# Dividing the attention output on GpSimd instead of VectorE, with a second copy of the transposed input and a new order at the end of each step

## The reference

```
x = x + attention(layernorm(x))       # 16 heads of 64, causal, own layernorm with weights inside
x = x + ffn(layernorm(x))             # sigmoid encoder, router over 8 experts (top 2), experts, decoder
attention: q, k, v = x Wq + bq, x Wk + bk, x Wv + bv
           p = softmax(q k^T / 8, causal);  z = p v;  out = z Wo + bo
```

## Time and profile before

| | |
|---|---|
| median of 3 runs | 1163.17 us (1163.03 to 1163.51) |
| profiled execution | 1161.71 us, its span 1160.0 us |
| TensorE, VectorE, ScalarE, GpSimd busy | 90%, 78%, 61%, 57% of the span |
| TensorE clock granted, mean | 0.975 |
| DMA, share of 16 engines | 64.3% on the one queue used |

### The profile page before, as it was taken

The page is one execution under the profiler, slowest core; times in us unless marked ns, Lnnn a source line. Parts: engine busy times, 40 slices in busy tenths (PEclk is TensorE's granted clock), DMA queues, the critical chain, the costliest instruction groups (busy, mean ns, idle before and its releaser), DMA issues.

```text
span 1160.0 us, 51334 instructions
## 1 busy us (share of the span) xinstructions
PE 1039.1 (90%) x19852; PEld 772.4 (67%) x19852; DVE 903.1 (78%) x2180; ACT 703.5 (61%) x1474; POOL 658.7 (57%) x658
## 2 busy tenths in 40 slices
PE   5689999999999999999999999999999848699984
PEld 3577777777777777777777777777777636354542
DVE  6878888888888888888888888888888863547573
ACT  4656666666666666666666666666666542577664
POOL 5766666666656666666666666665666202244644
PEclk9999999999999999999999999999999877899998
DMA  7677777777777776777777777777777740132422
GB/s 172 164 182 172 174 169 173 169 173 172 171 167 181 165 175 168 168 168 168 168 170 174 175 172 170 171 169 172 173 173 170 179 91 21 38 84 47 91 50 60
DMA packets 127279, 173.06 MB, mean 149 GB/s; under 512 B 46096, under 2 KB 57360, under 8 KB 127248
## 3 DMA queue, kind: packets, MB, share of 16 engines
q1 hardware_dynamic: 127248, 172.67, 64.3%
HBM read 117.67 MB, written 21.36 MB: 120 GB/s over the span
## 4 chain that ended last, share of the span: by engine, by line
PE 71%; DVE 13%; DMA 5%; issue 5%; ACT 3%; SPq 2%; POOL 1%; DVEq 0%; POOLq 0%; ACTq 0%
PE ZB L658 25%; PE SPS L641 12%; PE SPS L642 10%; PE ZB L626 8%; DVE PTZ L918 4%; PE ZB L631 4%; DMA XTB<-xt_scratch 4%; PE ZB L666 3%; DVE SSB L975 2%; SPq L416 2%; PE SPS L817 1%; PE SPS L791 1%; PE ZB L832 1%; PE ZB L826 1%; PE ZB L809 1%
## 5 line engine op out<-in xcount | busy, mean ns | idle before, releaser
L975 DVE CUSTOM_DVE_ANT_0 SSB<-SPS,MASK 128x640 f32<-128x640 f32 (+7 forms) x512 | 372.0, 745 | 124.6 <-PE SPS L642 111.1
L641 PE MATMUL SPS<-KHP,QS 128*128 (+2 forms) x768 | 326.2, 430 | 33.5 <-DVE NM L975 28.7
L658 PE MATMUL ZB<-PTZ,VR 32*64 32x256 f32 (+2 forms) x16384 | 322.7, 295 | 21.4 <-DVE PTZ L918 19.0
L1278 ACT ACTIVATE PRL<-SSB,NM 128x640 f32<-128x640 f32 (+3 forms) x256 | 253.3, 989 | 144.9 <-DVE NM L975 144.4
L658 PEld LDWEIGHTS ZB<-PTZ,VR 32*64 32x64 f32 x16384 | 271.5, 131 | 69.3 <-issue 53.9
L483 POOL TENSOR_TENSOR X<-X,OT 128x512 f32 (+1 forms) x64 | 81.9, 1279 | 342.3 <-ACT OT L1288 333.9
L642 PE MATMUL SPS<-KLP,QS 128*128 (+2 forms) x768 | 261.4, 348 | 0.0
L918 DVE STREAM_TRANSPOSE PTZ<-PRL 128x640 f32<-128x640 f32 (+3 forms) x256 | 258.6, 1030 | 0.0
L1278 ACT ACTIVATE PRS<-SSB,NM 128x128 f32<-128x128 f32 (+3 forms) x256 | 142.5, 559 | 154.4 <-DVE NM L975 154.4
L641 PEld LDWEIGHTS SPS<-KHP,QS 128*128 128x128 f32 x768 | 145.3, 189 | 110.9 <-issue 47.2
L466 POOL TENSOR_TENSOR QS<-RAW,QS 64x512 fp32r<-64x512 f32 x128 | 165.3, 1292 | 10.3
(11 more groups left out here) (167 smaller groups left out, 999.6 us busy)
## 6 DMA issues: line engine op xcount, KB each, us to landing
VR<-v_scratch SPq DMA_DIRECT2D x256, 256.0 KB, 5.6
KHP<-KHP SPq DMA_DIRECT2D x64, 256.0 KB, 3.2
KLP<-KLP SPq DMA_DIRECT2D x64, 256.0 KB, 3.9
v_scratch<-V SPq DMA_DIRECT2D x32, 512.0 KB, 7.7
RSB<-rcp_scratch SPq DMA_DIRECT2D x64, 256.0 KB, 4.0
XTB<-xt_scratch SPq DMA_DIRECT2D x62, 256.0 KB, 3.4
VR<-gate_scratch SPq DMA_DIRECT2D x16, 512.0 KB, 5.9
WQK<-in_W_q SPq DMA_DIRECT2D x33, 64.0 KB, 3.2
```

Source lines behind the costliest of these rows:

```text
L641: pe.matmul(SP_[n % 2][:, c0:c0 + wc], q, kh[:, c0:c0 + wc], start=True, stop=False)
L658: last = pe.matmul(ZB[h * DH:(h + 1) * DH, i, kt * TR:QT * TR], VR[rows, j, kt, h * DH:(h + 1) * DH], turned_block(h, kt, j, rows), start= ...
L975: v.tensor_tensor_reduce(out=SSB[n % 2][:, 0:w], in0=SP_[n % 2][:, 0:w], in1=MASK[:, S - w:S], scale=1.0, scalar=BIG, op0=ALU.add, op1=ALU ...
L1278: act.activation(exps_of(n), SSB[n % 2][:, 0:w], ACT.Exp, bias=NM[:, col:col + 1], scale=-1.0, accum_out=L[:, col:col + 1]).then_inc(exp_d ...
```

## The change

- The division: ScalarE copies Z from PSUM to the ZN tiles in two copies of 128x512 (`act_z`, after the exponential of unit 11), and GpSimd multiplies ZN by RSB in place in two operations of 128x512 (`divide`, ahead of `add_out(0)`). `out_of(g)` waits for division g only; `v_of` waits for the first copy. The four VectorE operations go.
- V of the step ahead is computed from its own copy of the transposed input, XW, from step 2 on; a transfer of 512 KB a step is added for it (`stage_xv`), ahead of the reciprocals in the queue. XTB's transfers move ahead of V's first spread and wait only for the queries and keys computed from XTB.
- The reciprocals' second transfer also waits for `split_q` of the step, which stands behind the division that read RSB.
- TensorE: `v_of(0)`, `v_of(1)` after scores 13, then scores 14 and 15, then the output products (before: scores 13 and 14, V, output, scores 15).
- VectorE: turn 8 ahead of mask 11 (before: behind it), mask 15 ahead of turn 12, turn 13 of the step behind ahead of mask 0.
- ScalarE: the first output copy after the exponential of unit 14, the second after that of unit 15 (before: after those of 13 and 14, with the exponential of 15 in the next step behind the first evacuation of `qk`).

```diff
+        def stage_xv(sp, it):
+            sp.wait_ge(v_filled, it * 2)
+            sp.nop(nofuse=True)
+            sp.dma_start(XW[:, :], xt_dram[:, bass.ds(((it // HP) % B) * S, S)]).then_inc(xv_staged, DMA)
 ...
+            if isinstance(it, int) and it == STEPS - 1:
+                sp.wait_ge(zn_done, it * 2)
+            else:
+                sp.wait_ge(q_split, it * 4 + 8)
 ...
+        def divide(gp, it, g):
+            gp.wait_ge(z_copied, it * 2 + 2)
+            gp.wait_ge(r_spread, it * (2 * DMA) + 2 * DMA)
+            gp.nop(nofuse=True)
+            z = ZN[g].rearrange("p (t i r) -> p i t r", i=P // TR, r=TR)
+            gp.tensor_tensor(z, z, RSB[:, g, :].rearrange("p (i t r) -> p i t r", t=TC, r=TR), ALU.mult).then_inc(zn_done, 1)
 ...
                 if not first:
+                    divide(gp, it - 1, 0)
+                    divide(gp, it - 1, 1)
                     add_out(gp, it - 1, 0)
 ...
-            scores(13, 14)
+            scores(13)
             v_of(0)
             v_of(1)
+            scores(14, 15)
             out_of(0)
             out_of(1)
-            scores(15)
 ...
-            turn(6, 7)
+            turn(6, 7, 8)
             stats(5)
             mask(11)
-            turn(8)
             mask(12)
 ...
-            for k in range(4):
-                zn(k)
             turn(9)
 ...
             mask(14)
+            mask(15)
             turn(12)
-            mask(15)
 ...
+        def act_z(act, it, k):
+            banks = slice(2 - k * 2, 4 - k * 2)
+            act.wait_ge(pv_done, it * QT + QT)
+            act.activation(PTZ[:, QT * 9 * P:QT * 9 * P + 2 * CH].rearrange("p (q i r) -> p i q r", i=P // TR, r=TR)[:, banks],
+                           ZB[:, banks, 0:QT * TR].rearrange("p i (q r) -> p i q r", r=TR), ACT.Copy).then_inc(z_copied, 1)
 ...
-            exps_to(11, 13)
+            exps_to(11, 12)
+            if not first:
+                act_z(act, it - 1, 0)
+                act_z(act, it - 1, 1)
+            exps_to(12, 13)
             v_of(0)
             exps_to(13, 14)
             v_of(1)
-            out_of(0)
             exps_to(14, 15)
+            out_of(0)
+            exps_to(15, 16)
             out_of(1)
```

More of the change, by code:

```diff
@@ L214, in build_program @@
         x_staged = [sem(f"x_staged{c}") for c in range(2)]
+        xv_staged = sem("xv_staged")
         keys_spread = [sem(f"keys_spread{c}") for c in range(2)]
@@ L222, in build_program @@
         v_early = sem("v_early"); v_late = sem("v_late")
-        pv_done = sem("pv_done"); zn_done = sem("zn_done")
+        pv_done = sem("pv_done"); z_copied = sem("z_copied"); zn_done = sem("zn_done")
         bias_filled = sem("bias_filled"); bias_ready = sem("bias_ready")
@@ L287, in stage_x @@
             part = bass.ds(((it // HP) % B) * S + c * CH, CH)
-            sp.wait_ge(v_filled, it * 2 + c - 1)
+            if isinstance(it, int) and it == 2:
+                sp.wait_ge(v_filled, 3 + c)
+            else:
+                sp.wait_ge(qk_filled, it * 4)
+                sp.nop(nofuse=True)
+            sp.dma_start(XTB[:, c * CH:(c + 1) * CH], xt_dram[:, part]).then_inc(x_staged[c], DMA)
+        def stage_xv(sp, it):
+            sp.wait_ge(v_filled, it * 2)
             sp.nop(nofuse=True)
-            sp.dma_start(XTB[:, c * CH:(c + 1) * CH], xt_dram[:, part]).then_inc(x_staged[c], DMA)
+            sp.dma_start(XW[:, :], xt_dram[:, bass.ds(((it // HP) % B) * S, S)]).then_inc(xv_staged, DMA)
         def stage(sp, it):
@@ L368, in body @@
                 else:
+                    if not last:
+                        stage_xv(sp, it + 1)
                     spread_sums(sp, it - 1)
@@ L378, in body @@
                     spread(sp, it + 1, 1 - par, 1)
+                    if not first:
+                        stage_x(sp, it + 2, 0)
+                        stage_x(sp, it + 2, 1)
                 spread_v(sp, it, half, par, 0)
-                if not last:
+                if first:
                     stage_x(sp, it + 2, 0)
@@ L574, in _ @@
             norm_in(1, 1)
+            divide(gp, STEPS - 1, 0)
+            divide(gp, STEPS - 1, 1)
             add_out(gp, STEPS - 1, 0)
@@ L628, in pe_v @@
         def pe_v(pe, it, s, bank):
+            xt = XTB if isinstance(it, int) and it < 2 else XW
             for k in range(TC):
                 t = s * TC + k
-                last = pe.matmul(bank[:, k * P:(k + 1) * P], XTB[:, t * P:(t + 1) * P],
+                last = pe.matmul(bank[:, k * P:(k + 1) * P], xt[:, t * P:(t + 1) * P],
                                  WV[:, bass.ds((it % HP) * 2, 2), :].rearrange("p h e -> p (h e)"), start=True, stop=True)
@@ L663, in pe_out @@
         def pe_out(pe, it, g, bank):
-            pe.wait_ge(zn_done, it * 4 + 4)
+            pe.wait_ge(zn_done, it * 2 + g + 1)
             for i in range(TC):
@@ L710, in v_of @@
                 else:
-                    pe.wait_ge(zn_done, it * 4 - 2)
+                    pe.wait_ge(z_copied, it * 2 - 1)
+                    if s == 0:
+                        pe.wait_ge(xv_staged, it * DMA)
                 pe_v(pe, it + 1, s, ZB[:, 2 + s, :])
@@ L925, in dve_reciprocal @@
             v.transpose(RT[:, :, :].rearrange("p g c -> p (g c)"), RCP[:, :, :].rearrange("p g c -> p (g c)")).then_inc(rcp_turned, 1)
[L927 to L934, removed]
         def dve_bias(v):
@@ L1036, in back @@
                     dve_reciprocal(v, it - 1, 1 - par)
-            def zn(k):
-                if not first:
-                    dve_zn(v, it - 1, k)
+            turn_back(13)
             mask(0)
@@ L1048, in dve_step @@
                 v.memset(ONES, 1.0).then_inc(zeroed, 1)
-            turn_back(13)
             turn_back(14)
@@ L1210, in _ @@
             dve_low(v, 0, 0)
-            for k in range(4):
-                dve_zn(v, it, k)
             gates_1(v, 0)
@@ L1319, in act_step @@
                 qk(0)
-                act_exp(act, it - 1, 1 - par, UNITS - 1)
                 exps_to(0, 1)
@@ L1350, in act_step @@
             exps_to(14, 15)
+            out_of(0)
+            exps_to(15, 16)
             out_of(1)
-            if last:
-                act_exp(act, it, par, UNITS - 1)
         @block.scalar
@@ L1431, in _ @@
             turn_of(1)
+            act_z(act, STEPS - 1, 0)
+            act_z(act, STEPS - 1, 1)
             act_out(act, STEPS - 1, 0, Z)
```

## The result

| | before | after |
|---|---|---|
| median | 1163.34 us (1163.03 to 1171.34) | 1184.86 us (1183.12 to 1187.07) |
| span of the profiled execution | 1160.0 us | 1181.4 us |
| busy: TensorE, VectorE, ScalarE, GpSimd | 90%, 78%, 61%, 57% | 88%, 73%, 62%, 63% |
| granted clock, mean | 0.975 | 0.972 |

The change makes the kernel slower, by 1.8%: ratio 1.0178 [1.0147, 1.0209]. The forecast was 1179.9 us, its range 1163.5 to 1192. VectorE did lose its work (868.0 us busy in all), and the end of each step did not come sooner.

What follows compares the result with a forecast made beforehand. Three chains meeting at the value products' start bound a step, TensorE having only 1.11 us to give. Loop +15.3, with the ends +16.7, on 1161.71; median 1.46 higher: 1179.9 us, range 1163.5 to 1192 without rivals 1 and 3.

Steps and rivals of the forecast that it cites:

- The mechanism: Loop step's end: first output copy, behind exponential 14, ends 1.08 us later, delaying second copy and splits; +0.73 a step.
- The second chain: Loop step's end: second output copy, third key product, mask 2, turn 15 at 632.05; value products could start at 633.43.
- One sign: Sign of being right: V or its weight load waits over 1 us for the last evacuation or turn 15.
- Division: Mid-step: ScalarE's copies 0.5 us each, GpSimd's divisions 1.28 each, inside its idle 9.13 us; output products not held.
- Rival 2: GpSimd's permuted division is slow, 2.56 us each, delaying output products: 29.35 a step, 1191.5 us; chance 0.07.
- Masks beside GpSimd: VectorE's masks (one PSUM, one SBUF operand) keep their length beside GpSimd; over 1.2 us at 1024 columns means wrong.
- Rival 3: GpSimd slows VectorE's masks beside the divisions, factor 3, delaying mask 14 by 1.7 us: 1229 us; chance 0.02.
- The size of a step: Loop: value products start at 633.50, +0.73 us a step, period 28.95; stated error 0.2 us a step.
- The slack before: Kernel before: chain from first output copy through splits and evacuation allows V at 632.42, against 632.77: 0.35 us.
- Rival 1: First copy's end moves less than 0.35 us, TensorE's end decides: 28.11 a step, 1155.9 us; chance 0.13.
- XTB: Transfer issued some 9 us earlier: key products' waits, 0.18 us a step, go; step 1's wait of 3.55 gives -0.9.
- The end: Behind the loop: last step -1.3 us, after the loads -0.5, tail +3.6 as the output product waits for copies and division.

Runs made afterwards that it cites:

- Experiment 9: Kernel before with only the copy XW for V and the moved XTB transfers: 1157.33 us, ratio 0.9935.
- Experiment 1: Changed kernel with the first output copy ahead of exponential 14 again: 1175.30 us, ratio 1.0093 to the kernel before.
- experiment 2: Changed kernel with two OT tiles, so the second output copy doesn't wait for the first addition; GpSimd's order stays: 1223.48 us.
- 6: Changed kernel with two OT tiles and, on GpSimd, the splits of queries 2 and 3 ahead of both additions: 1162.31 us.
- 7: The kernel of 6 with both output copies ahead of exponential 15 in addition: 1150.78 us, ratio 0.9875 to the kernel before.
- Experiment 4: Changed kernel with the transfers as before: V from XTB, no XW, XTB's transfer between V's spreads: 1190.09 us.
- experiment 5: Changed kernel with the division on VectorE again, straight from PSUM, everything else as changed: 1211.68 us.
- experiment 10: The kernel of 8 with turn 15 of the step behind ahead of mask 2: 1130.63 us, ratio 0.9729 to the kernel before.
- 8: The kernel of 7 with, in the tail, Z's copies one turn earlier and the router's exponential ahead of the output copies: 1144.03 us, ratio 0.9827.
- experiment 3: The kernel of experiment 2 (changed kernel with two OT tiles) run once more, four executions: 1228.67 us, ratio 1.0541.

## Why the prediction was right, and what it got wrong

**The mechanism held.** The loop step is longer because the first output copy comes later, behind exponential 14, and two things hang on it. Experiment 9, with the transfers alone, has 28.23 a step and the changed kernel 29.14, so the rest of the change costs 0.9. Experiment 1 shows that the copy's place costs 0.40 of it, 2 and 6 what the splits behind the addition do, 6 and 7 what the second copy holds. Experiment 4 excludes the added transfers. The second chain was right too: turn 15 starts 27.57 us behind V where 27.50 was forecast (632.05 - 604.55). The periods that the chains gave for 1, 4, 5, 6, 7, 9 and 10 came within 0.1 us. How the 0.9 divides between TensorE's and ScalarE's new order isn't shown, as no run changed TensorE's alone. One sign was over-stated: V was to wait over 1 us and waited 0.80, since `qk(2)` takes 0.77 of TensorE's time ahead of it.

**Division: right.** The permuted operation takes 1.28 us a tile (80.8 us for 64), the lower of the two bounds. Rival 2 is out. `v_of` and the output products weren't held.

```profile
L505 POOL TENSOR_TENSOR PTZ<-PTZ,RSB 128x512 f32<-128x512 f32 x64 | 80.8, 1285 | 166.8 <-ACT PTZ L1306 166.8
```

**Masks beside GpSimd: right, though a sign of being wrong came true.** Mask 15 takes 1.22 us beside a split of GpSimd's in experiment 10 and 1.22 in the changed kernel, where GpSimd idles from 637.02 to 640.35:

```profile
607.31 1.22 DVE L1001 CUSTOM_DVE_ANT_0 SSB<-SPS,MASK 128x1024 f32<-128x1024 f32 x1
...
607.71 1.28 POOL L486 TENSOR_TENSOR QS<-RAW,QS 64x512 fp32r<-64x512 f32 x1
```

```profile
638.27 1.22 DVE L1001 CUSTOM_DVE_ANT_0 SSB<-SPS,MASK 128x1024 f32<-128x1024 f32 x1
```

Rival 3 is out, and so is the wide reading of the rule on shared SBUF interfaces in the Trainium skill, GPSIMD Engine Reference, "Key points": beside GpSimd the masks, with one PSUM and one SBUF operand, kept their length, as its wording has it. But the masks of 1024 columns are longer than before, 1.22 us in the mean against 1.19, and so over the 1.2 that the prediction named as a sign against it. Mask 12 lengthened too, 1.09 against 1.05, with GpSimd idle beside it, so GpSimd isn't the cause. The cause stays open.

**The size of a step: low by 0.19, and that is where the sum's miss lies.** The forecast was 28.95, measured 29.14. The term was "With 0.08 to TensorE, my estimate by the other lags": V started 0.24 us after the evacuation's end (646.69 to 646.93; in the step before 617.55 to 617.78, 0.23). The other joints of the chain were right to 0.05 (6.83 in all against 6.72). The rest is that exponential 14 started 20.61 us behind V and not 20.49: mask 13 started 0.05 us later than reckoned, and masks 13 and 14 were 0.04 and 0.03 longer. By 28 steps the miss is 5.2 us, within the error of 0.2 a step that was stated. The other stretches missed by +1.4, -0.8, +0.2, -1.7 and +0.4 us, which nearly cancel.

The slack before was smaller than the prediction has it, for the same reason. ScalarE's row in the kernel before shows that the last evacuation ended at 632.38:

```profile
630.28 2.10 ACT L1257 ACTIVATE RAW<-ZB,BQKS,QKSCALE 128x512 f32<-128x512 f32 x3
```

With 0.24 to TensorE V could have started at 632.62, so the slack was about 0.15 us and not 0.35 (an estimate, as the 0.24 is from the changed kernel).

**Rival 1 (the copy chain has room) was wrong by its own point.** The first copy's end moved by 22.32 - 21.15 = 1.17 us behind V (21.15 from 625.70 - 604.55), more than the slack of 0.35. With the copies' chains cut, experiments 6 and 7 have 28.35 and 27.91 a step, on both sides of its 28.11.

**XTB: right in the loop, wrong at its start.** The 0.18 a step exist (0.17 in experiment 9). In step 1 the product did start 1.18 us sooner, but the rest of the step gave it back: the key product took 2.01 us where the earlier trace rows have 1.12.

```profile
54.27 2.01 PE L658 MATMUL ZB<-XTB,WQK 128*128 128x512 f32 x2 [2.06 <-DMA XTB<-xt_scratch]
55.29 1.20 PE L674 MATMUL SPS<-KHP,QS 128*128 x1
```

```profile
54.27:56.30 2.03, 2.03 (x4) 0.99 (x5) 1.61 (x2) 0.87 (x2) 1.89 (x3) 0.52 1.07 186
```

The granted clock was 0.52 there; before, after a longer wait (3.55 us), it was 1.00. The first two stretches together came out at +0.16 us where -0.4 was forecast.

**The end.** The last two intervals gave 3.3 us where 1.8 was forecast, the tail cost 4.05 for 3.6. The tail's mechanism is read from the start of the router's exponential behind the last mark: 23.68 us before, 26.85 after, so +3.17 where +3.6 was forecast. Moved ahead of the output copies (experiments 8 and 10) it starts at 19.74 and 18.1. The whole stretch from the last mark to the end agrees. Division on VectorE: 196.46, 194.27 (experiment 9) and 195.1 (experiment 5). Division on GpSimd: 200.51, 202.97, 199.72, 203.12, 205.33, 204.44 and 201.46 (the changed kernel, experiments 1 to 4, 6 and 7). Exponential and copies moved ahead: 193.95 and 193.97. Its rows are ScalarE's and TensorE's, beside the earlier trace rows:

```profile
1005.22 0.60 ACT L1312 ACTIVATE OT<-ZB 128x512 f32<-128x512 f32 x1 [3.53 <-PE ZB L699]
1007.25 0.60 ACT L1312 ACTIVATE OT<-ZB 128x512 f32<-128x512 f32 x1 [1.43 <-POOL X L511]
1007.74 0.22 ACT L1431 ACTIVATE PRS<-PRS 128x32 f32<-128x32 f32 x1
```

```profile
1003.16 3.68 PE L699 MATMUL ZB<-WO,PTZ 128*128 128x128 f32 x16 [3.09 <-POOL PTZ L505]
```

The seven values with the division on GpSimd differ by 5.6 us. They go with the granted clock of the stretch, from 0.94 in the shortest to 0.91 and 0.90 in the two longest; the kernels at 193.95 to 195.1 have 0.95. So a difference of a few us in the tail, of one execution each, isn't the mechanism's alone. Why the last interval gained 2.17 and not 0.5 stays open.

## What to carry to other kernels

Work taken from an engine pays only where that engine's end sets a step; look first at what else ends there within a few tenths of a us, and sum the chain over the engines with each joint between them at what the trace shows for it (0.05 to 0.30 us here). When work is put into an engine that runs strictly in order, place the short operation that others wait for (here a copy of 0.6 us) ahead of the long one that waits for somebody itself. Before a change that costs 1.8% is dropped, look for the part of it that costs: here the division and the copy were sound, the order around them was not. The version that gains 2.7% also has five further edits: two OT tiles, the splits ahead of the additions, both copies ahead of exponential 15, the tail, and turn 15. What these would give to the kernel before, with its division on VectorE, was not tried, so the 2.7% isn't the division's.

## What the runs showed of the hardware that was not expected

A wait of the same length is not always followed by the same clock. In experiment 2 the 1.44 us ahead of V were followed by full clock for the first steps (3.50 us for the 128 products) and by 0.50 from about 210 us on (5.08 to 5.19 us), in every step after. In experiment 3 no loop step was free of it. In experiment 5 the wait of 1.52 us stood ahead of `qk(2)` and the one ahead of V was 0.85; all ran at full clock. In step 1 a wait of 3.55 us was followed by 1.00 and one of 2.06 us by 0.52. In experiment 2 TensorE's work and waits in the step ahead of the first fall (V at 209.66) are the same as in the step ahead of 180.52, where the clock stayed: 0.17, 0.43 and 1.45 us against 0.18, 0.43 and 1.44. So neither the length of the wait nor that step's work alone decides. What does was not tried, and stays open. TensorE's idle time in such a step is 0.17 + 0.43 + 1.44 = 2.04 us, in the changed kernel it is 0.77 + 0.43 + 0.80 = 2.00 us in three more even parts, without the fall; the fall costs 1.6 to 1.7 us a step.
